# A linear layer's bias: a product of ones and bias rows on TensorE, or an addition on GpSimd

## The reference

```
x = x + tanh(g_xattn[0]) * memory(ctx, layernorm(x))        # 4 rows shift into a memory
x = x + tanh(g_ffn[0])   * (xd @ wd.T + bias)               # xd, wd: block-quantised values, 32 to a block
x = x + tanh(g_xattn[1]) * attention(layernorm(x), ctx)     # 77 keys per batch
x = x + tanh(g_ffn[1])   * experts(layernorm(x))            # 8 experts of 512 x 2048, capacity 1280
```

## Time and profile before

| | before |
|---|---|
| median of 3 runs | 2247.3 us |
| profiled execution | 2244.2 us, span 2242.5 us |
| PE busy | 1988.4 us (89%) |
| DVE busy | 1055.7 us (47%) |
| ACT busy | 797.9 us (36%) |
| POOL busy | 681.2 us (30%) |
| POOL, L621 (X<-X,gbias) | 16 instructions, 73.3 us |
| token stage | about 77 to 897 us |
| expert stage | about 901 us to the end |

### The profile page before, as it was taken

One profiled execution on the slowest core, in us unless ns is written; L12 is line 12 of the kernel. 1 busy time (PEld: TensorE's weight loads), 2 busy tenths in 40 slices (PEclk: granted clock), 3 DMA queues, 4 the chain that ended last, 5 costly groups with the idle time before them and its releaser, 6 DMA issues.

```text
span 2242.5 us, 35473 instructions
## 1 busy us (share of the span) xinstructions
PE 1988.4 (89%) x11356; PEld 1694.7 (76%) x11357; DVE 1055.7 (47%) x2310; ACT 797.9 (36%) x1548; POOL 681.2 (30%) x587
## 2 busy tenths in 40 slices
PE   2358889989988985399999999999999999999997
PEld 2146677767776764288898999899889899889987
DVE  4177898899889743614242113211422413312241
ACT  2134656665566543314132113211422312311241
POOL 0143344343434212515243113311522412311250
PEclk9669999999999985599999999999999999999999
DMA  6221333233333223714243013300421501411130
GB/s 169 100 68 38 112 120 137 104 127 118 131 112 124 74 77 132 231 39 141 79 131 101 19 37 102 117 28 28 140 90 42 173 24 63 139 33 37 45 116 18
DMA packets 152195, 208.42 MB, mean 93 GB/s; under 512 B 12782, under 2 KB 78574, under 8 KB 152149
## 3 DMA queue, kind: packets, MB, share of 16 engines
q1 hardware_dynamic: 111077, 114.14, 15.9%
q0 software_dynamic: 15728, 43.38, 6.2%
q10 hardware_dynamic: 25344, 50.33, 6.2%
HBM read 140.98 MB, written 68.37 MB: 93 GB/s over the span
## 4 chain that ended last, share of the span: by engine, by line
PE 56%; issue 1%; DMA 1%; POOL 1%; ACT 1%; DVE 0%; POOLq 0%; DVEq 0%; ACTq 0%
PE bank L1546 23%; PE bank L1554 22%; PE bank L1519 5%; PE bank L1499 5%; PE bank L1477 1%; PE bank L1508 1%; POOL w_lo L1291 0%; DMA tgu<-t_d,idx_tu 0%; PE bank L1483 0%; ACT w_hi L1411 0%; ACT w_hi L1412 0%; DMA out_dram<-obu,idx_xu 0%; POOLq L1209 0%; DVE xg L1704 0%; POOL out_dram L1281 0%
## 5 line engine op out<-in xcount | busy, mean ns | idle before, releaser
L1640 DVE SCALAR_TENSOR_TENSOR hT_lo<-bank,hT_hi 128x256 fp32r<-128x256 f32 x352 | 149.2, 424 | 656.9 <-ACT hT_hi L1442 634.3
L1442 ACT ACTIVATE hT_hi<-bank 128x256 fp32r<-128x256 f32 x352 | 135.2, 384 | 749.3 <-PE bank L1546 735.3
L1546 PE MATMUL bank<-inT_hi,w_lo 128*128 128x256 f32 x1408 | 398.5, 283 | 0.0
L1546 PE MATMUL bank<-inT_lo,w_hi 128*128 128x256 f32 x1408 | 398.3, 283 | 0.0
L1546 PE MATMUL bank<-inT_hi,w_hi 128*128 128x256 f32 x1408 | 396.8, 282 | 0.0
L1554 PE MATMUL bank<-w_hi,hT_hi 128*128 128x512 f32 x704 | 279.9, 398 | 0.0
L1546 PEld LDWEIGHTS bank<-inT_hi,w_hi 128*128 128x128 f32 x1408 | 269.0, 191 | 13.3
L1546 PEld LDWEIGHTS bank<-inT_lo,w_hi 128*128 128x128 f32 x1408 | 269.0, 191 | 12.0
L1554 PE MATMUL bank<-w_lo,hT_hi 128*128 128x512 f32 x704 | 277.7, 394 | 0.0
L1554 PE MATMUL bank<-w_hi,hT_lo 128*128 128x512 f32 x704 | 274.1, 389 | 0.0
L1546 PEld LDWEIGHTS bank<-inT_hi,w_lo 128*128 128x128 f32 x1408 | 269.0, 191 | 0.0
(11 more groups left out here) (263 smaller groups left out, 3916.1 us busy)
## 6 DMA issues: line engine op xcount, KB each, us to landing
stage<-in_L_ffn_W_dram SPq DMA_DIRECT2D x256, 256.0 KB, 2.9
X<-in_x_dram SPq DMA_DIRECT2D x16, 1024.0 KB, 5.1
t_d<-tt ACTq DMA_DIRECT2D x16, 1024.0 KB
x_d<-x ACTq DMA_DIRECT2D x16, 1024.0 KB
out_dram<-y ACTq DMA_DIRECT2D x16, 1024.0 KB, 4.3
xs<-in_x_dram SPq DMA_DIRECT2D x16, 768.0 KB
cw<-in_L_xattn_conv_w_dram SPq DMA_DIRECT2D x1, 4096.0 KB, 33.9
xs<-in_x_dram SPq DMA_DIRECT2D x16, 128.0 KB
```

What stands on the lines that cost most here:

```text
L1442: act.activation(hT_hi[:, f % 4, :], hb[f % 4][:, 0:CN], ACT.Relu).then_inc(e_hh, 1)
L1546: last = pe.matmul(hb[f % 4][:, 0:CN], l[:, k, fs], r[:, k, :], start=(n == 0), stop=(n == 3 * KB - 1))
L1640: dve.scalar_tensor_tensor(out=hT_lo[:, f % 4, :], in0=hb[f % 4][:, 0:CN], scalar=0.0, in1=hT_hi[:, f % 4, :].bitcast(F32), op0=ALU.max, o ...
```

## The change

The bias is no longer added to X by POOL. Instead the set-up makes two small tiles of 33 rows: `one_rows`, all ones, and `bias_rows`, with the high part of the bias in row 0, the low part in row 32 and zeros elsewhere. Each linear group on PE gets the product of the two as its first term, so that the PSUM bank holds xd @ wd.T + bias; the gate is multiplied in by add_linear, as before. add_linear(0) waits for n1 to be read out of X (`a_n1`) in place of `g_xb`.

```diff
+    BR = 33
-        gbias = tb("gbias", [P, D], F32)
+        bias_rows = tb("bias_rows", [BR, D], F32R)
+        one_rows = tb("one_rows", [BR, P], F32R)
...
-            POOL_STEPS = 14
+            POOL_STEPS = 17
...
                 pool.memset(onesf[:, :], 1.0).then_inc(ready, 1)
+                pool.memset(pick[:, :], 0.0).then_inc(k_pool, 1)
+                pool.wait_ge(k_pool, 2)
+                pool.affine_select(out=pick[:, 0:1], in_=pick[:, 0:1], compare_op=ALU.not_equal, fill=1.0,
+                                   base=0, pattern=[[0, 1]], channel_multiplier=1).then_inc(k_pool, 1)
+                pool.affine_select(out=pick[:, 1:2], in_=pick[:, 1:2], compare_op=ALU.not_equal, fill=1.0,
+                                   base=-(BR - 1), pattern=[[0, 1]], channel_multiplier=1).then_inc(k_pool, 1)
...
                 act.preload_act_table_set("natural_log_exp_and_others")
+                act.activation(b_hi[:, :], fb_raw[0:BR, :], ACT.Copy).then_inc(k_act, 1)
+                act.wait_ge(ready, 1)
+                act.activation(one_rows[:, :], onesf[0:BR, :], ACT.Copy).then_inc(k_act, 1)
...
-                step("gbias", dve.tensor_scalar(gbias[:, :], fb_raw[:, :], gates[:, 2:3], None, ALU.mult))
+                dve.wait_ge(k_act, act_at["b_hi"])
+                dve.wait_ge(k_pool, POOL_STEPS)
+                step("b_lo", dve.tensor_tensor(b_lo[:, :], fb_raw[0:BR, :], b_hi[:, :].bitcast(F32), ALU.subtract))
+                after("b_lo")
+                step("b_pick", dve.tensor_scalar(b_lo[:, :], b_lo[:, :], pick[:, 1:2], None, ALU.mult))
+                after("b_pick")
+                step("b_rows", dve.scalar_tensor_tensor(out=bias_rows[:, :], in0=b_hi[:, :].bitcast(F32), scalar=pick[:, 0:1],
+                                                        in1=b_lo[:, :], op0=ALU.mult, op1=ALU.add))
...
-                    wait(pool, a_n1, T * (a + 1))
-                    wait(pool, g_x1, a + 1)
-                    settled(pool)
-                    pool.tensor_tensor(X[:, ds(r, T), :], X[:, ds(r, T), :],
-                                       gbias[:, :].unsqueeze(1).to_broadcast([P, T, D]), ALU.add).then_inc(g_xb, 1)
...
                     product(l_banks[j % 2][:, :],
-                            [term for k in range(KB) for term in
+                            [(one_rows[:, :], bias_rows[:, :])] + [term for k in range(KB) for term in
                              split_terms(xdT_hi[:, k, js], xdT_lo[:, k, js], wd_hi[:, k, :], wd_lo[:, k, :])]
                             ).then_inc(p_bm, 1)
...
                     if j == 0:
-                        wait(dve, g_xb, b + 1)
+                        wait(dve, a_n1, T * (b + 1))
```

More of the change, by code:

```diff
@@ L146, in flamingo_two_layers @@
             anyk = st("anyk", [P, B], F32)
+            b_hi = st("b_hi", [BR, D], F32R)
+            b_lo = st("b_lo", [BR, D], F32)
+            pick = st("pick", [BR, 2], F32)
             anyi = st("anyi", [P, B], F32)
@@ L176, in flamingo_two_layers @@
             w_init, w_comp, w_uq, w_cx = sem("w_init"), sem("w_comp"), sem("w_uq"), sem("w_cx")
-            DVE_STEPS = ["zero", "gbias", "kmf", "maskb", "kfree", "anyk", "anyi", "anyr", "gx",
+            DVE_STEPS = ["zero", "b_lo", "b_pick", "b_rows", "kmf", "maskb", "kfree", "anyk", "anyi", "anyr", "gx",
                          *[f"uw{k}" for k in range(KB)], *[f"cxT{k}" for k in range(KB)],
@@ L191, in flamingo_two_layers @@
             pe_at = {n: i + 1 for i, n in enumerate(PE_STEPS)}
-            ACT_STEPS = [*[f"uw{k}" for k in range(KB)], *[f"cxT{k}" for k in range(KB)],
+            ACT_STEPS = ["b_hi", "b_one", *[f"uw{k}" for k in range(KB)], *[f"cxT{k}" for k in range(KB)],
                          *[f"cxhi{b}" for b in range(B)], "xln", "xrs", *[f"wd{k}" for k in range(KB)],
@@ L259, in _ @@
                           allow_small_or_imprecise_dtypes=True).then_inc(k_pool, 1)
-                pool.wait_ge(k_pool, 10)
+                pool.wait_ge(k_pool, 13)
                 pool.affine_select(out=ident[:, :], in_=ident[:, :], compare_op=ALU.not_equal, fill=1.0,
@@ L482, in flamingo_two_layers @@
         s_xs, s_x, s_uq, s_cx, s_t, s_x3, s_y, s_slot = (sem("s_" + n) for n in ("xs", "x", "uq", "cx", "t", "x3", "y", "slot"))
-        g_x1, g_xb, g_xd = (sem("g_" + n) for n in ("x1", "xb", "xd"))
+        g_x1, g_xd = (sem("g_" + n) for n in ("x1", "xd"))
         a_u, a_n1, a_bh, a_n2, a_ch, a_uh, a_st, a_al, a_th, a_tt, a_tT, a_re, a_y = (
```

## The result

The changed kernel takes 2280.2 us (median of 4 runs, 2277.0 to 2283.1) beside 2247.6 us for the kernel before on the same chip: ratio 1.0146, 95% interval 1.0128 to 1.0165, so 33 us slower. I had forecast 2250.3 us with a range up to 2259. The profiled execution took 2281.4 us, span 2279.7, against 2244.2 and 2242.5.

The account below looks back on a forecast made before the run. The token stage's chain of waits was taken to count, PE and DVE both nearly full in the loop. 14.9 us of added PE products less 11.94 us of hold gave +2.95 us, 2250.3 us on the median, range 2243 to 2259.

Parts of the forecast that it names:

- The bias product: PE's linear groups: 64 added 33-row products at 0.233 us each, 0.93 us per step, 14.9 us in all.
- Rows did not matter between 77 and 128: PE's neighbouring products: 128-row ones follow after 0.234 us, the 77-row one after 0.24, so 0.233 was taken for 33 rows.
- rival 1: Start of each linear group on PE: 33-row product costs a restart, 0.10 us more each, +9.3, 2256.6 us; chance 0.25.
- My upper bound of 0.40 us: PE: most a bias product was taken to cost, its own duration with nothing overlapped; +13.6 us in total.
- The hold on a_m: DVE's a_m waits for POOL's gbias addition in 11 steps; removal gains 0.96 us in most looped steps, 11.94 in all.
- the distance of the up_lo: DVE, from start of up_lo(0) to start of up_lo(3): 14.4 us in looped steps once a_m is free.
- The set-up: Before the steps: extra ACT, DVE and POOL operations, at most 3.4 us, hidden by DVE's wait for xc; cost 0.
- Rival 4: Emptying pipeline from 860 us: a shift may move the granted clock's fall, −5 to +5 us, 2242 to 2255; chance 0.10.
- The expert stage must … last as long as before: Expert stage: a sign of the forecast, starting 3 us later with unchanged length.
- my sum says 2.95: All steps together: PE's added products less the returned hold make +2.95 us, or +0.13%.

Follow-up runs that it names:

- r65: The changed kernel with the two bias tiles 65 rows high instead of 33, added rows zero; 2254.4 us, ratio 1.0038.
- r64: The changed kernel with the two bias tiles 64 rows high instead of 33, added rows zero; 2281.0 us, ratio 1.0154.
- twice: The changed kernel with the 33-row bias product issued two times in a row per group, so bias counts double; 2277.6 us with other expert loads.
- last: The changed kernel with the 33-row bias product at the end of its group instead of the head; 2279.1 us, ratio 1.0142.
- none: The changed kernel without any bias product, the bias left out of the result; 2272.8 us with other expert loads.
- both: The changed kernel with POOL's gbias addition and its waits put back as well, so bias counts double; 2257.7 us with other expert loads.
- late: The kernel before with POOL's gbias addition moved behind its four multiplications of the quantised tile; 2255.5 us, ratio 1.0051.
- pad: The changed kernel with POOL's waits and a 128x1 memset of an unused tile in the addition's old place; 2278.2 us, ratio 1.0147.
- r65pad: The changed kernel with bias tiles 65 rows high, plus POOL's waits and a 128x1 memset in the addition's old place; 2250.2 us, ratio 1.0017.
- split: The kernel before with POOL's gbias addition done as four 128x512 additions after the next group's addition of xs to X; 2242.4 us, ratio 0.9985.

## Why the prediction was wrong

**The bias product (wrong, and it decides).** I took 0.233 us each and 14.9 in all, from 77-row and 128-row neighbours ("Rows did not matter between 77 and 128"). It measures 0.58 us, so 64 × 0.58 = 37 us. The step that failed is the carrying over of rows of 77 and 128 to a product of 33, which lies on the other side of a border between 64 and 65 rows. I had written that no row shows under 77 rows, and rival 1 had the right place ("where PE changes between 33 and 128 rows"), but its price was that of one restart, 0.10 us; the change costs 0.35 us, paid on entering and on leaving. My upper bound of 0.40 us, a product's own duration, was no bound: a load that is not pulled ahead adds to it. r65 and r64 show the border, twice that it is the change which costs, last that it isn't the start of a group.

**The hold on a_m (right).** a_m is 0.16 us and the distance of the up_lo 14.4, both as written, and none measures 0.95 us for the looped step against the 0.96 forecast. Added to the true price of the product it gives the looped step: −0.96 + 4 × 0.58 = +1.36, and 44.30 + 1.36 = 45.66. The sum of the two terms is sound, but it doesn't say who earned what: with the product in, `both` shows that the hold had all but gone in the looped steps, so there the removal of the addition was worth nothing.

**The set-up (right).** The first a_m starts at 87.92 us against 88.18.

**The clock (wrong).** Rival 4 looked for a shift only in the emptying pipeline. In the loop, the three longer steps cost 48.29 + 47.17 + 48.21 − 3 × 45.66 = 6.7 us. The sum is 37.1 − 11.9 (product and hold) + 6.7 = 31.9, against 32.25 measured for the token stage. It also fits stretch by stretch: up to a_m of step 6 the terms give 9.5 us and the trace 10.4, from there to step 15 it is 18.6 and 18.8, behind that 3.7 and 3.4, and the set-up gives 0.3 back. What decides whether a step has a fall stays open. Every variant has some and before has none. Nearly all begin 19 to 21 us behind the start of a_m, when PE has been busy for 2.0 to 2.8 of the last 4 us (the exceptions are three in late, behind its long waits for comp_d). But that stretch is in every step: in the looped steps of before, too, PE is busy in the worst 4 us for only 1.9, and no fall follows. So idle time in it isn't enough to bring a fall.

**"The expert stage must … last as long as before" (wrong).** It took 5.0 us longer; in pad, where the gather is not late, it took 0.4 longer. With it the span's difference is 32.25 + 5.0 = 37.2 us.

**The forecast with its own price.** r65, whose product does cost 0.23 us, ends the token stage 4.9 us late, one fall of 1.5 us included, where my sum says 2.95. r65pad, which has no late gather either, is 3.4 us slower than before by the medians. Even so it is no gain: it trades POOL's addition, which costs 0.95 us per step through a_m, for 0.95 us on PE.

## What to carry to other kernels

Before adding a small product to a dense run of large ones, look whether its operands stay on the same side of 64 rows as their neighbours'; if not, pad them with zero rows to 65 (r65: 26 us less for one constant, with neighbours of 77 and 128 rows). Where an engine's operation holds a short one on another engine, moving it can be cheaper than giving its work to the engine that is the bound (split against r65), but list what is queued behind its new place: late lost there what split kept. A duration from a row is a bound only for the kinds of operations in that trace, and 64 repetitions make an error of 0.35 us into 22.

## What the runs showed that was not expected

- A product of 33 or 64 rows between products of 77 or 128 rows costs 0.58 us instead of 0.23; the second of two of 33 rows in a row costs 0.23.
- The granted clock can fall once in every step of a loop at the same place, and cost 1.0 us in each (split, 44.35 us); in the step before the first fall, the same instructions took 43.34 us.
- With one addition and its waits gone from each copy of a step in its program, POOL began its first gather of the next stage 4.3 to 5.3 us later, with a packet of an instruction queue in the gap; one small instruction with its waits put back removed the gap.
